# Rotary products and sums by halves of the tokens in a one-core vision tower

## The reference, cut to what matters

```python
qkv = (x @ w_qkv).reshape(B, S, 3, N_HEADS, D_K)
q, k, v = ...
out_even = x_even * cos - x_odd * sin     # applied to q and to k
out_odd  = x_odd * cos + x_even * sin
scores = einsum('bhqd,bhkd->bhqk', q, k) * D_K ** (-0.5) + bias
attn = softmax(scores); out = einsum('bhqk,bhkd->bhqd', attn, v)
```

## Time and profile before

| | us |
|---|---|
| median of 3 runs | 273.88 (272.88 to 273.96) |
| the profiled execution's own time | 274.31 |
| its span, first to last instruction | 272.3 |
| PE busy in the span | 242.8 (89%) |
| DVE busy | 186.6 (69%) |
| ACT busy | 62.5 (23%) |
| POOL busy | 54.7 (20%) |

### The profile page before, as it was taken

The page is one execution under the profiler, slowest core; times in us unless marked ns, Lnnn a source line. Parts: engine busy times, 40 slices in busy tenths (PEclk is TensorE's granted clock), DMA queues, the critical chain, the costliest instruction groups (busy, mean ns, idle before and its releaser), DMA issues.

```text
span 272.3 us, 4922 instructions
## 1 busy us (share of the span) xinstructions
PE 242.8 (89%) x1992; PEld 205.9 (76%) x1992; DVE 186.6 (69%) x467; ACT 62.5 (23%) x116; POOL 54.7 (20%) x71
## 2 busy tenths in 40 slices
PE   0997975788868999899999899899979999999996
PEld 0996645677633588889889899888868888888763
DVE  1838297778886259999999999799968767511100
ACT  3701136353453241313122734100000000000000
POOL 5014055124322523315042520000000000000000
PEclk9999999999965899999999999999999999999999
DMA  7970000211003261161124520200000000000000
GB/s 250 387 241 0 0 1 2 103 60 32 18 19 94 63 216 39 31 202 41 41 79 153 159 76 0 92 0 2 0 19 2 0 22 0 0 22 0 19 2 12
DMA packets 14806, 17.01 MB, mean 62 GB/s; under 512 B 848, under 2 KB 12992, under 8 KB 14784
## 3 DMA queue, kind: packets, MB, share of 16 engines
q1 hardware_dynamic: 13776, 15.70, 17.6%
q10 hardware_dynamic: 1008, 1.00, 1.0%
HBM read 15.48 MB, written 1.21 MB: 61 GB/s over the span
## 4 chain that ended last, share of the span: by engine, by line
PE 54%; DVE 36%; ACT 4%; issue 3%; ACTq 1%; DVEq 0%; POOL 0%
PE ps L1091 23%; PE ps L1054 9%; PE ps L1113 5%; PE ps L846 4%; DVE topi L719 3%; PE ps L995 3%; DVE big L818 3%; DVE top L716 3%; PE ps L1088 3%; DVE big L570 2%; DVE xn L530 2%; PE ps L921 2%; PE ps L962 2%; PE ps L871 2%; DVE stats L522 1%
## 5 line engine op out<-in xcount | busy, mean ns | idle before, releaser
L1091 PE MATMUL ps<-ue,big 128*128 128x256 f32 (+1 forms) x320 | 72.3, 381 | 1.4 <-DVE big L818 1.4
L1091 PEld LDWEIGHTS ps<-ue,big 128*128 128x128 f32 (+1 forms) x320 | 57.2, 182 | 12.1 <-DVE big L818 1.8
L1054 PE MATMUL ps<-hn_hi,de_hi 128*128 128x296 f32 x128 | 40.7, 318 | 2.1 <-ACT big L497 1.1
L818 DVE TENSOR_TENSOR big<-ps,big 128x1024 f32<-128x1024 f32 (+1 forms) x19 | 22.7, 1197 | 26.9 <-PE ps L1113 26.2
L1054 PE MATMUL ps<-hn_lo,de_hi 128*128 128x296 f32 x128 | 38.3, 300 | 0.0
L1054 PE MATMUL ps<-hn_hi,de_lo 128*128 128x296 f32 x128 | 38.2, 298 | 0.0
L497 ACT ACTIVATE big<-ps 128x592 f32<-128x592 f32 x32 | 21.1, 665 | 44.5 <-PE ps L1054 44.4
L1054 PEld LDWEIGHTS ps<-hn_hi,de_hi 128*128 128x128 f32 x128 | 24.1, 188 | 4.5 <-DVE actT L765 1.9
L1054 PEld LDWEIGHTS ps<-hn_lo,de_hi 128*128 128x128 f32 x128 | 24.1, 188 | 1.2 <-issue 1.2
L1054 PEld LDWEIGHTS ps<-hn_hi,de_lo 128*128 128x128 f32 x128 | 24.1, 188 | 0.0
L704 DVE TENSOR_TENSOR late<-eqx,wsel 128x2048 f16<-128x2048 f16 (+1 forms) x19 | 22.7, 1197 | 0.7
(11 more groups left out here) (127 smaller groups left out, 386.4 us busy)
## 6 DMA issues: line engine op xcount, KB each, us to landing
de<-in_down_t SPq DMA_DIRECT2D x16, 256.0 KB, 2.9
ue<-in_up_e SPq DMA_DIRECT2D x4, 1024.0 KB, 6.9
big<-in_patches SPq DMA_DIRECT2D x6, 296.0 KB, 5.6
big<-in_w_tok ACTq DMA_DIRECT2D x6, 128.0 KB, 5.7
big<-in_w_qkv SPq DMA_DIRECT2D x1, 768.0 KB, 9.0
h_scratch<-big SPq DMA_DIRECT2D x5, 111.0 KB
late<-in_keys_bd SPq DMA_DIRECT2D x1, 512.0 KB, 9.9
downT<-in_wdown_t SPq DMA_DIRECT2D x1, 512.0 KB, 9.2
```

What stands on the lines that cost most here:

```text
L818: chain(nc.vector.tensor_tensor(dst, pv, dst, ALU.mult), g_ready)
L1054: last = mm(ps[:, 2 + 2 * (e % 2) + a, 0:HALF], half[:, (e // 2) % SPLITS, k, own], src[:, k, a * HALF:(a + 1) * HALF], start=(n == 0), st ...
L1091: last = mm(acc, sil[:, e, j * 128:j * 128 + Q * v], ue[:, e, :], start=False, stop=(e == EX - 1))
```

## The change

The four products of a rotation and its sums are made for one half of the tokens at a time. `pe_qk` is raised for each half of keys and queries, so it counts to 4. DVE's order becomes: key products of half 0, key sums of half 0, key products of half 1, key sums of half 1, query products of half 0, query sums of half 0, query products of half 1, query sums of half 1. The query sums are cut by half, by side and by the place of an image in its group (`im` = 0, 1, 2), with one more for each side of `q_left`.

In PE's queue the second projection of query half 0 moves behind the two of key half 1, so that nothing stands any more between the transpose of group 5 and the wait for ACT's copy of it. The waits on `kT_ready`, `rope_done` and `q_ready` get the new counts. POOL and ACT still spread keys of both halves at once.

```diff
-                pool.wait_ge(kT_ready, a + 1)
+                pool.wait_ge(kT_ready, a + 3)
...
-                act.wait_ge(kT_ready, a + 1)
+                act.wait_ge(kT_ready, a + 3)
...
-            def rotate(t):
-
-                dve.wait_ge(pe_qk, t + 1)
+            def rotate(t, half):
+
+                dve.wait_ge(pe_qk, 2 * t + half + 1)
+                at = 4 * t + 2 * half
+                cols = slice(half * HALF, (half + 1) * HALF)
                 for i, (odd, table) in enumerate(((0, cosb), (1, sinb), (0, sinb), (1, cosb))):
-                    src = ps[:, 4 * t + odd:4 * t + 4:2, 0:HALF].rearrange("p a (b s) -> p a b s", s=S)
                     behind()
...
+                    chain(nc.vector.tensor_tensor(rot[:, i, cols].rearrange("p (b s) -> p b s", s=S),
+                                                  ps[:, at + odd, 0:HALF].rearrange("p (b s) -> p b s", s=S),
+                                                  table, ALU.mult), rope_done if i == 3 else dve_chain)
+                behind()
+
+            def key_sums(half):
+
+                cols = slice(half * HALF, (half + 1) * HALF)
+                for a, (i, op) in enumerate(sides):
+                    chain(nc.vector.tensor_tensor(kT[:, a, cols], rot[:, i, cols], rot[:, i + 1, cols], op), kT_ready)
+
+            def query_sums(half):
...
+                for a, (i, op) in enumerate(sides):
+                    for im in range(PER):
...
+                        groups = [g for g in range(FULL) if half * HALF <= g * ROWS + im * S < (half + 1) * HALF]
+                        g0, g1 = groups[0], groups[-1] + 1
...
+                        chain(nc.vector.tensor_tensor(window[:, g0:g1, 0:S], v[0], v[1], op), q_ready)
+                    if half == 1:
+                        chain(nc.vector.tensor_tensor(q_left[:, a, :], rot[:, i, whole:T], rot[:, i + 1, whole:T], op),
+                              q_ready)
+
+            rotate(0, 0)
+            key_sums(0)
+            rotate(0, 1)
+            key_sums(1)
+            rotate(1, 0)
             dve.wait_ge(s_zero, 1)
...
+            query_sums(0)
+            rotate(1, 1)
+            query_sums(1)
...
-            for odd in range(2):
-                rope_input(0, 0, odd)
+            rope_input(0, 0, 0)
+            rope_input(0, 0, 1).then_inc(pe_qk, 1)
             tokens_T(3)
             tokens_T(4)
             pe.wait_ge(xn_ready, NG)
             rope_input(1, 0, 0)
             tokens_T(5)
-            rope_input(1, 0, 1)
             pe.wait_ge(xnT_ready, NG)
             rope_input(0, 1, 0)
             rope_input(0, 1, 1).then_inc(pe_qk, 1)
+            rope_input(1, 0, 1).then_inc(pe_qk, 1)
             rope_input(1, 1, 0)
             rope_input(1, 1, 1).then_inc(pe_qk, 1)
 
-            pe.wait_ge(rope_done, 1)
+            pe.wait_ge(rope_done, 2)
...
-            pe.wait_ge(rope_done, 2)
+            pe.wait_ge(rope_done, 4)
             for u in range(4):
                 values(u)
-            pe.wait_ge(q_ready, 4)
+            pe.wait_ge(q_ready, 2 * (2 * PER + 1))
```

More of the change, by code:

```diff
@@ L559, in _ @@
             token_norm(NG - 1)
-            cosb = con[:, C_COS:C_COS + S].unsqueeze(1).unsqueeze(1).broadcast_to([128, 2, B // 2, S])
-            sinb = con[:, C_SIN:C_SIN + S].unsqueeze(1).unsqueeze(1).broadcast_to([128, 2, B // 2, S])
-            def rotate(t):
-                dve.wait_ge(pe_qk, t + 1)
+            cosb = con[:, C_COS:C_COS + S].unsqueeze(1).broadcast_to([128, B // 2, S])
+            sinb = con[:, C_SIN:C_SIN + S].unsqueeze(1).broadcast_to([128, B // 2, S])
+            sides = ((0, ALU.subtract), (2, ALU.add))
@@ L567, in rotate @@
+            def rotate(t, half):
+                dve.wait_ge(pe_qk, 2 * t + half + 1)
+                at = 4 * t + 2 * half
+                cols = slice(half * HALF, (half + 1) * HALF)
                 for i, (odd, table) in enumerate(((0, cosb), (1, sinb), (0, sinb), (1, cosb))):
-                    src = ps[:, 4 * t + odd:4 * t + 4:2, 0:HALF].rearrange("p a (b s) -> p a b s", s=S)
                     behind()
-                    chain(nc.vector.tensor_tensor(rot[:, i, :].rearrange("p (a b s) -> p a b s", a=2, s=S),
-                                                  src, table, ALU.mult), rope_done if i == 3 else dve_chain)
+                    chain(nc.vector.tensor_tensor(rot[:, i, cols].rearrange("p (b s) -> p b s", s=S),
+                                                  ps[:, at + odd, 0:HALF].rearrange("p (b s) -> p b s", s=S),
+                                                  table, ALU.mult), rope_done if i == 3 else dve_chain)
@@ L572, in rotate @@
                 behind()
[L574 to L578, removed]
-            dve.wait_ge(s_zero, 1)
[L580 to L587, removed]
+            def key_sums(half):
+                cols = slice(half * HALF, (half + 1) * HALF)
+                for a, (i, op) in enumerate(sides):
+                    chain(nc.vector.tensor_tensor(kT[:, a, cols], rot[:, i, cols], rot[:, i + 1, cols], op), kT_ready)
@@ new lines, in query_sums @@
+            def query_sums(half):
+                first, last = ((0, HALF // ROWS), (HALF // ROWS, FULL))[half]
+                whole = FULL * ROWS
+                for a, (i, op) in enumerate(sides):
+                    for im in range(PER):
+                        window = qpad[:, a, :].rearrange("p (i x) -> p i x", i=PER)[:, im, 0:whole]
+                        window = window.rearrange("p (g r) -> p g r", g=FULL)
+                        groups = [g for g in range(FULL) if half * HALF <= g * ROWS + im * S < (half + 1) * HALF]
+                        g0, g1 = groups[0], groups[-1] + 1
+                        v = [rot[:, i + n, 0:whole].rearrange("p (g r) -> p g r", g=FULL)[:, g0:g1, im * S:(im + 1) * S]
+                             for n in range(2)]
+                        chain(nc.vector.tensor_tensor(window[:, g0:g1, 0:S], v[0], v[1], op), q_ready)
+                    if half == 1:
+                        chain(nc.vector.tensor_tensor(q_left[:, a, :], rot[:, i, whole:T], rot[:, i + 1, whole:T], op),
+                              q_ready)
```

## The result

The changed kernel takes 275.44 us (median of 5 runs, 274.91 to 276.87) against 273.88: a ratio of 1.0066 with a 95% interval of 1.0038 to 1.0095. It is slower, by 1.6 us by the medians and by 1.0 to 2.6 by the interval. The profiled execution took 274.91 us (its span is 273.1), 0.60 more than the profiled one of before. It is the fastest of its five, while the profiled one of before, at 274.31, is slower than the runs behind its median, so the two traces show less of the loss than the medians do.

A forecast was written before the change was run, and what follows sets the result against it. DVE's chain to the first scores was taken as the bound, with at most 4.81 us of idle time usable. Balance 0.0 plus clock 2.5 on the median 273.88 gave 276.4 us, range 272.7 to 277.8.

The forecast's parts named there:

- The keys: DVE's key work by halves: half 0 summed by 31.0, half 1 products from 32.25, fourth key sum at 35.1.
- The lost cover of ACT's copy: In PE's queue, query half 0 no longer covers ACT's copy of group 5: costs PE 0.4 us.
- The turns: Six query sums of half 0 alternate with POOL's two casts and two subtractions, from 37.12 to 41.35; bounds 38.1 and 41.4.
- the plain alternation of the prediction: At the port shared by DVE and POOL, query sums and POOL instructions take strict turns, three each way seen before.
- rival (b): DVE gets two query sums per turn, ending at 40.2: 272.7 us, or 275.2 if the clock falls; chance 0.25.
- The balance without the clock: First scores at 45.7 against 45.73: the port takes back what the halves win, 0.0 us; 273.9 with clock kept.
- The clock: PE's pause of 4.0 us before the transposes halves its clock from 43.5 to 49.0: +2.5 us.
- the low bound of 1.7: Least cost of the clock's fall: only PE's transposes slow, 1.94 less 0.25 hidden, +1.7 us.
- That a shift reaches the end whole: PE and DVE hand over round by round after the softmax, so a shift of first scores should reach the end whole.
- Rival (c): The port lock hardly bites: half 0's query sums end at 38.1, scores 2.4 us earlier, clock kept, 271.5 us; chance 0.13.

The follow-up runs named there:

- the kernel with the pause filled: Changed kernel plus eight projections nobody reads in PE's pause between the value projection and values(0): 273.48 us, 0.9986 of the kernel before.
- with POOL's rounds first: Changed kernel with POOL's first two rounds of casts and subtractions moved ahead of its key head: 270.07 us, 0.9875 of the kernel before.
- with the products first: Changed kernel with the query products of half 1 put ahead of all fourteen query sums: 270.55 us, 0.9902 of the kernel before.
- with keys by halves alone: Changed kernel with query products and sums whole as before; keys by halves and the new projection order stay: 270.3 us, 0.9868 of the kernel before.
- keys by halves with POOL's rounds first: Keys by halves, queries whole, and POOL's first two rounds ahead of its key head: 270.34 us, 0.9878 of the kernel before.
- the profiled execution with two sums: Changed kernel with query sums cut at whole groups, six in place of fourteen, two after the first products: 272.69 us, 0.996 of the kernel before.

## Why the prediction was right, and what it sized wrong

**The keys.** Right: key sums of half 0 by 31.06 with the later opening taken off (forecast 31.0), key products of half 1 at 32.30 (32.25), the fourth key sum at 35.14 (35.1). The lost cover of ACT's copy cost 0.37 us (PE goes on at 29.99, with the opening taken off, instead of 29.62), and 0.4 was said.

**The turns.** Right in size, and the term that decides. The query sums of half 0 ended at 41.69, or 41.41 with the opening taken off; the forecast was 41.35. The order of turns was not the plain alternation of the prediction. Single sums, as the rows of their line in the changed kernel tell them, took 740, 261, 1301, 673, 262 and 1295 ns. The line in two short windows (shortest, median and longest in ns, first and last start):

```profile
L595 DVE TENSOR_TENSOR ue<-big x2: 261/500/740, 37.5 to 38.2; 128x111 f32<-128x111 f32 x2
...
L595 DVE TENSOR_TENSOR ue<-big x1: 1301/1301/1301, 38.4 to 38.4; 128x74 f32<-128x74 f32 x1
```

After each cast two sums got in, as rival (b) held, but the first cast came in ahead of the first sum (it ran unblocked, in 0.60 us), so all four POOL instructions got in after all. That the end fits the forecast to 0.06 us is therefore partly luck. The first-to-start rule of the Trainium skill (SBUF — State Buffer, "SBUF: two separate sides") agrees with the two sums after a cast. At the first turn it does not settle the order: the sum's row begins 0.01 us before the cast's, yet the cast ran first, and POOL's key head before it was at work until 37.58, past both starts. The blocking for the rest of an instruction agrees with the sums of 1301 and 1295 ns, each beside a subtraction.

**The balance without the clock.** Right: forecast 0.0, and the kernel with the pause filled is at 0.9986 of before, with an interval (0.9964 to 1.0008) that includes 1.

**The clock.** The mechanism was right: a pause of 4.39 us (forecast 4.0), and the granted clock at 0.50 from its end. The term of +2.5 was too large for what arrived at the first softmax, 1.25 us, which is also below the low bound of 1.7 (all sixteen transposes slow). The step that failed is the length taken over from the end of the attention, 5.5 us at half speed; here the clock was back after 3.4, at 47.24, and the transposes lost 1.60 us. In time the term looks larger: the filled kernel stands at 0.9986 of before and the changed one at 1.0066, so the clock costs 0.8% or 2.2 us (2.0 by the medians, 275.44 less 273.48). The two intervals together leave about 1.2 to 3.2 us (an estimate), which holds 2.5 and only just 1.25. The trace may also show a mild case: the profiled execution, the fastest of the five, had a mean granted clock of 0.969, and three of the other four had 0.962 or 0.963, so these stood longer at half speed than the trace shows. What makes up the rest between 1.25 and 2.0 was not isolated.

**That a shift reaches the end whole.** Only roughly. In the profiled executions the stretch from first softmax to first expert product took 46.1 us before, 45.3 in the changed kernel, 45.2 with POOL's rounds first and 44.75 with the products first, and everything after it 178.2 to 178.5 in these four. So the profiled execution of the changed kernel stood 1.53 behind at the softmax and only 0.76 at the first expert product. In this stretch the clock is at half speed for a time in every kernel: from 77.4 to 91.1 us in the kernel before, from 74.6 to 78.0 and again from 81.4 to 91.6 in the changed one, and from 77.1 to 87.3 with keys by halves alone. The windows in which it rises, in the kernel before and with keys by halves alone:

```profile
90.00:92.00 2.00, 2.00 (x5) 0.68 (x3) 0.00 (x0) 0.07 (x1) 1.92 (x3) 0.73 0.00 0
...
86.00:88.00 2.00, 2.00 (x4) 0.86 (x3) 0.07 (x1) 0.59 (x1) 1.35 (x2) 0.68 0.03 10
```

Counted from the last normalisation, the softmax came 2.7 us earlier with POOL's rounds first, 2.5 with keys by halves alone and 1.6 with the products first, yet these kernels are 3.9, 3.9 and 3.4 us faster. That a shorter time at half speed accounts for the extra 1.2 to 1.8 us is argued, not isolated by a run.

The times on record speak for part of it. Of the 37 runs of the kernel before that stood beside the experiments, 28 had a mean granted clock of 0.974 or 0.975 and a median of 274.16 us, and nine had 0.980 or 0.981 and a median of 272.97: in one and the same kernel a longer time at half speed goes with 1.2 us more. All six runs with keys by halves alone had 0.981, and so had five of six with POOL's rounds first and with the products first. Held against those nine, the medians of these runs are 2.7, 3.0 and 2.5 us faster, which is nearer to the 2.5, 2.7 and 1.6 of the softmax. It is not the whole account: keys by halves with POOL's rounds first had 0.975 in four of its six runs and was as fast as the others.

Rival (c) names what would have made the change a gain, and the kernel with POOL's rounds first is that case: sums in 1.1 us, the clock kept in this stretch, and the softmax 2.7 us earlier (2.4 forecast for the scores).

## What to carry to other kernels

Before cutting a VectorE instruction with two SBUF operands into pieces, look at what POOL has in its queue at that moment: a short piece can pay a whole POOL instruction as its turn. Here six sums of about 0.2 us met four POOL instructions and took 4.2 us. Put work that others wait for (here the products that free PSUM for PE) ahead of work that may be blocked; the same instructions in another order were worth 1.6% (1.0066 to 0.9902). And when a pause of TensorE grows, price the clock as well as the wait: a fill of idle products won back 2 us here without doing anything useful.

## What the runs showed of the hardware

The length of PE's pause alone does not tell whether the clock falls. After 2.47 us in the profiled execution with two sums it stayed at 1.00. Behind a later pause of 2.21 us it fell 2.3 us after the pause's end there, at 77.7, and 0.2 us after it in the kernel before. With that pause filled it fell at 83.8 us, behind pauses of 0.9 and 1.1 us, and in the changed kernel it fell at 74.6, behind none above 0.44 us since 62 us. Once down it stayed at half for 3.4 us in the changed kernel's first fall and for some 13.6 us at the end of the attention in the kernel before (77.4 to 91.1).

With POOL's rounds first, the pair of key sums of half 0 took 1.70 us instead of 0.84, blocked by a subtraction:

```profile
29.73 1.70 DVE L586 TENSOR_TENSOR slots<-big 128x296 f32<-128x296 f32 x2
31.81 1.97 DVE L577 TENSOR_TENSOR big<-ps,con 128x296 f32<-128x296 f32 x4 [0.38 <-PE ps L897]
```

That cost nothing, because DVE stood idle behind them anyway until the second half's keys came (0.38 us were left). A turn costs only where the blocked engine is late.
